# Layer 2 of a four-layer attention stack: probabilities turned by TensorE, or split into 16-bit planes and turned by a DMA

## The reference

```python
xq = _layernorm(q, ln1_w, ln1_b)
Q = jnp.einsum('btc,hdc->bhtd', xq, Wq)
K = jnp.einsum('bsc,hdc->bhsd', k, Wk)
V = jnp.einsum('bsc,hdc->bhsd', v, Wv)
scores = jnp.einsum('bhtd,bhsd->bhts', Q, K) * D ** (-0.5)
wei = jax.nn.softmax(scores, axis=-1)
o = jnp.einsum('bhts,bhsd->bhtd', wei, V)
o = o.transpose(0, 2, 1, 3).reshape(q.shape[0], q.shape[1], H * D)
q1 = q + o @ Wproj.T + bproj
h = _layernorm(q1, ln2_w, ln2_b)
return q1 + jax.nn.relu(h @ W1.T + b1) @ W2.T + b2
```

## Time and profile before

| | |
|---|---|
| Median of 3 runs | 4999.22 us (4997.36 to 5001.67) |
| The profiled execution | 5001.85 us, span 5000.1 us |
| PE / PEld busy | 4600.5 us (92%) / 3401.8 us (68%) |
| DVE / ACT / POOL busy | 2935.6 us (59%) / 2821.5 us (56%) / 2007.6 us (40%) |
| Mean granted TensorE clock | 0.957 |
| DMA queue q1 | 279216 packets, 155.99 MB, 12.9% of 16 engines |

### The profile page before, as it was taken

The page is one execution under the profiler, slowest core; times in us unless marked ns, Lnnn a source line. Parts: engine busy times, 40 slices in busy tenths (PEclk is TensorE's granted clock), DMA queues, the critical chain, the costliest instruction groups (busy, mean ns, idle before and its releaser), DMA issues.

```text
span 5000.1 us, 86857 instructions
## 1 busy us (share of the span) xinstructions
PE 4600.5 (92%) x32032; PEld 3401.8 (68%) x32032; DVE 2935.6 (59%) x6466; ACT 2821.5 (56%) x8969; POOL 2007.6 (40%) x3876
## 2 busy tenths in 40 slices
PE   8999999876877777789999999999999999999998
PEld 5666666655656556567777777777777777777777
DVE  6566556566656665664544454445445766676665
ACT  4555555688888888863333333333334666666664
POOL 3333333466565665642222222222223444444443
PEclk9999999988889888899999999999999999999999
DMA  2000000133333333331000000000000100000000
GB/s 82 21 24 21 25 23 21 51 67 62 64 62 61 62 67 56 68 69 39 11 14 14 14 11 14 14 14 11 14 23 23 37 15 21 21 18 16 20 17 7
DMA packets 279638, 161.54 MB, mean 32 GB/s; under 512 B 244528, under 2 KB 261168, under 8 KB 277808
## 3 DMA queue, kind: packets, MB, share of 16 engines
q1 hardware_dynamic: 279216, 155.99, 12.9%
HBM read 82.53 MB, written 14.68 MB: 19 GB/s over the span
## 4 chain that ended last, share of the span: by engine, by line
PE 83%; ACT 8%; POOL 3%; DVE 2%; issue 2%; DMA 2%; SPq 0%; ACTq 0%; POOLq 0%; DVEq 0%
PE ring L1340 49%; PE ring L1287 11%; PE score L1273 11%; ACT e L1460 5%; PE ring L1322 3%; PE ring L1315 3%; PE ring L1329 2%; DMA probs<-steps 2%; POOL e L1850 1%; PE ring L1284 1%; POOL e L1847 1%; PE ring L1305 1%; ACT work L1521 1%; PE ring L1355 1%; DVE nmax L1595 1%
## 5 line engine op out<-in xcount | busy, mean ns | idle before, releaser
L1850 POOL TENSOR_SCALAR e<-e,rsum 112x375 f32<-112x375 f32 (+1 forms) x2048 | 1067.4, 540 | 2214.8 <-DVE rsum L1602 2178.9
L1500 ACT COPY probs<-ring 125x336 f32<-125x336 f32 (+1 forms) x971 | 400.1, 448 | 1648.2 <-PE ring L1287 1533.9
L1595 DVE TENSOR_REDUCE nmax<-score 112x2 f32<-112x750 f32 (+1 forms) x1152 | 1064.7, 951 | 420.6 <-PE score L1273 420.5
L1460 ACT ACTIVATE e<-score,nmax 112x375 f32<-112x375 f32 (+1 forms) x2048 | 1039.1, 539 | 42.5 <-DVE nmax L1595 38.2
L1340 PE MATMUL ring<-h,weights 128*128 128x224 f32 x3840 | 876.0, 369 | 30.0 <-ACT work L1521 24.9
L1273 PE MATMUL score<-keys,q 64*112 64x375 f32 (+2 forms) x3584 | 608.4, 494 | 232.4 <-ACT e L1460 229.6
L1340 PEld LDWEIGHTS ring<-h,weights 128*128 128x128 f32 x3840 | 724.9, 197 | 104.4 <-ACT work L1521 33.7
L1287 PEld LDWEIGHTS ring<-consts,e 112*125 112x125 f32 x4608 | 584.5, 188 | 230.8 <-issue 178.9
L1287 PE MATMUL ring<-consts,e 112*125 112x112 f32 x4608 | 645.4, 279 | 4.6 <-POOL e L1850 2.6
L1340 PE MATMUL ring<-weights,ctx 128*125 128x512 f32 (+3 forms) x1536 | 588.4, 516 | 0.0
L1273 PEld LDWEIGHTS score<-keys,q 64*112 64x112 f32 (+2 forms) x3584 | 233.0, 166 | 509.2 <-ACT e L1460 287.1
(11 more groups left out here) (123 smaller groups left out, 5104.9 us busy)
## 6 DMA issues: line engine op xcount, KB each, us to landing
ctx<-ctx_t SPq DMA_DIRECT2D x128, 375.0 KB, 3.1
out_t<-x SPq DMA_DIRECT2D x64, 224.0 KB, 1.9
x<-out_t SPq DMA_DIRECT2D x48, 224.0 KB, 2.6
weights<-weights SPq DMA_DIRECT2D x7, 1024.0 KB, 6.2
probs<-steps SPq DMA_TRANSPOSE x320, 2.7
x<-x_t SPq DMA_DIRECT2D x16, 224.0 KB, 2.6
weights<-weights SPq DMA_DIRECT2D x1, 3328.0 KB, 12.3
weights<-weights SPq DMA_DIRECT2D x1, 2304.0 KB, 9.4
```

Of the source, the lines that this page charges most:

```text
L1460: ins = nc.scalar.activation(e_of(u)[:, n * width:(n + 1) * width], score_bank(u)[0:S, n * width:(n + 1) * width], ACT.Exp, bias=minus, sc ...
L1500: ins = nc.scalar.copy(dst, src)
L1595: ins = dve.tensor_reduce(to, src, AX, ALU.max, negate=True)
L1850: ins = nc.gpsimd.tensor_scalar(mine, mine, rsum[0:S, slot(u), n:n + 1], 0.0, ALU.mult, ALU.add)
```

## The change

In layer 2 the turns on TensorE are gone. After `weigh`, a new step `split` on GpSimd (L1946 of the changed kernel, two instructions for each pair) reads the float32 probabilities as pairs of 16-bit words and writes all low halves and all high halves into `halves`, three slots of 12 blocks of 128 columns. A transposing DMA on SyncE's queue (L1996) moves the 12 blocks into `planes`, two slots. A new step `merge` on VectorE (L1734) or ScalarE (L1537) interleaves the two planes again into float32 words in `probs`. The context is cut into chunks of 128, 128 and 119 keys in place of three of 125, in `cv` and in `pv`. Layer 1's `steps` now share their memory with `halves`, which is cleared once at the start as `steps` was.

```diff
+WORDS = (2, )
+SPLIT_BY = ("G",)
+SPLITS = 3
+PLANES = 2
...
-                if o.layer != 1:
+                if o.layer != 1 and not self.in_words(o):
                     self.turn_of[u] = self.job(p.index + lag + 0.1 * i, "turn", o.layer, o.s, o.b, 0, "VA", u)
             if p is o.pairs[-1] and len(o.pairs) == (2 if o.attn == "self" else 4):
-                self.pv_of[o] = self.job(p.index + (3.4 if o.layer == 1 else lag + 0.5), "pv", o.layer, o.s, o.b, o.half, PV_BY[o.layer], o)
+                self.pv_of[o] = self.job(p.index + (3.4 if o.layer == 1 else (4.5, 0, 3.9, 4.3)[o.layer] if self.in_words(o) else lag + 0.5), "pv", o.layer, o.s, o.b, o.half, PV_BY[o.layer], o)
+    def halves_before(self, p):
+
+        i = self.nth_halved[p]
+        found = [self.halved[i - SPLITS]] if i >= SPLITS else []
...
+    def in_words(self, o):
+        return o.layer in WORDS and o.attn == "cross"
...
+            if self.in_words(o_):
+                by = SPLIT_BY[self.nth_halved[p] % len(SPLIT_BY)]
+                self.add("split", p, by, 1.7, p.index + 1.4)
+                self.add("flip", p, "D", 4.2, p.index + 1.6)
+                self.add("merge", p, "VA", 1.45, p.index + 2.4)
...
+        elif kind == "split":
+            yield "weigh", x
+            for p in self.halves_before(x):
+                yield "flip", p
+        elif kind == "merge":
+            yield "flip", x
+            for o in self.probs_before(x.octet):
+                yield "job", self.pv_of[o]
+        elif kind == "flip" and self.in_words(x.octet):
+            yield "split", x
+            i = self.nth_halved[x]
+            if i >= PLANES:
+                yield "merge", self.halved[i - PLANES]
...
-        steps = sb("steps", [P, STEPSLOTS, 8 * P], BF16)
+        halves = sb("halves", [P, SPLITS, 4 * CHUNKS * P], U16)
+        steps = halves[:, :, :].rearrange("p a n -> p (a n)")[:, 0:STEPSLOTS * 8 * P].bitcast(BF16).rearrange(
+            "p (a n) -> p a n", a=STEPSLOTS)
+        planes = sb("planes", [P, PLANES, 4 * CHUNKS * S], U16)
...
+        def split(eng, wait, p):
+            wait.wait_ge(weighed, nth["weigh", p])
+            for before in plan.halves_before(p):
+                flip_done(wait, before)
+            to = halves_of(p).rearrange("p (h a n) -> p h a n", h=2, a=2)
+            src = e[0:S, pair_slots(p), 0:T].bitcast(U16).rearrange("p a (n h) -> p h a n", h=2)
+            return [(to[:, h, :, 0:T], src[:, h, :, :]) for h in range(2)]
+
+        def merge(wait, p):
+            flip_done(wait, p)
+            wait.done([plan.pv_of[o] for o in plan.probs_before(p.octet)])
+            to = merged_of(p).rearrange("p a n -> p (a n)").bitcast(U16).rearrange("p (m h) -> p m h", h=2)
+            return to, planes_of(p).rearrange("p (h m) -> p m h", h=2)
...
-            return (P * c, min(T, P * c + P)) if layer == 1 else (R * c, R * c + R)
+            return (P * c, min(T, P * c + P)) if layer == 1 or layer in WORDS else (R * c, R * c + R)
...
+                elif kind == "merge":
+                    to, src = merge(wait, x_)
+                    nc.scalar.copy(to, src).then_inc(merged["A"], 1)
...
+                elif plan.in_words(before.octet):
+                    wait.wait_ge(halved[plan.split_by[before]], nth["split", before])
...
+                elif kind == "merge":
+                    to, src = merge(wait, x_)
+                    dve.tensor_copy(to, src).then_inc(merged["V"], 1)
...
+                if kind == "split":
+                    for to, src in split(pool, wait, x_):
+                        ins = nc.gpsimd.tensor_scalar(to, src, 1.0, 0.0, ALU.mult, ALU.add)
+                    ins.then_inc(halved["G"], 1)
+                    continue
...
+                        sp.dma_start(planes_of(p).rearrange("p (a n) -> p a n", n=S), halves_of(p),
+                                     transpose=True).then_inc(turned[n % FLIPS], 16)
```

More of the change, by code:

```diff
@@ L224, in place_attention @@
         self.turn_of, self.pv_of = {}, {}
+        self.halved = [p for p in self.pairs if self.in_words(p.octet)]
+        self.nth_halved = {p: i for i, p in enumerate(self.halved)}
         self.ones = [p for p in self.pairs if p.octet.layer == 1]
@@ L481, in before @@
                     yield "eight", self.pairs[x.index - ES // 2]
+                elif self.in_words(self.pairs[x.index - ES // 2].octet):
+                    yield "split", self.pairs[x.index - ES // 2]
                 else:
@@ L828, in arrange @@
                     step.x.clip_by, step.x.clip_nth = e, counts[e, "clip"]
+                if step.kind == "merge":
+                    self.by[step.x] = e
+                if step.kind == "split":
+                    self.split_by[step.x] = e
                 if step.kind == "job":
@@ L1078, in probs_of @@
             dt = BF16 if o.layer == 1 else F32
-            if o.layer == 1 and not is_own(o):
-                return part(probs[:, o.index % 2, :], 0, [8, CHUNKS, S], dt)[chunk_rows(1, c), col, c, :]
+            if o.layer == 1 and not is_own(o) or plan.in_words(o):
+                return part(probs[:, o.index % 2, :], 0, [8, CHUNKS, S], dt)[chunk_rows(o.layer, c), col, c, :width]
             if is_own(o):
@@ L1295, in tensor_heads @@
                     flip_done(wait, p)
+            elif plan.in_words(o):
+                for p in o.pairs:
+                    wait.wait_ge(merged[plan.by[p]], nth["merge", p])
             else:
@@ L1372, in tensor_product @@
                     half, c = j.m // 3, j.m % 3
-                    return product(ps[0:R, :], ((src[:, k, c * R:(c + 1) * R], wt[:, k, half * 512:half * 512 + 512])
-                                                for k in range(KC)))
+                    a, z = chunk(2, c)
+                    return product(ps[0:z - a, :], ((src[:, k, a:z], wt[:, k, half * 512:half * 512 + 512])
+                                                    for k in range(KC)))
                 for i, c in enumerate((0, 1) if j.m == 0 else (2,)):
@@ L1624, in vector_program @@
                     ins.then_inc(ctx_scaled, 1)
+                elif kind == "split":
+                    for to, src in split(dve, wait, x_):
+                        ins = dve.tensor_copy(to, src)
+                    ins.then_inc(halved["V"], 1)
+                elif kind == "merge":
+                    to, src = merge(wait, x_)
+                    dve.tensor_copy(to, src).then_inc(merged["V"], 1)
                 elif kind == "eight":
@@ L1627, in vector_program @@
                     wait.wait_ge(weighed, nth["weigh", p])
-                    i = plan.nth_of_one[p]
-                    if i >= STEPSLOTS:
-                        flip_done(wait, plan.ones[i - STEPSLOTS])
+                    for before in plan.steps_before(p):
+                        flip_done(wait, before)
                     if is_own(p.octet):
@@ L1875, in sync_program @@
                     n = nth["flip", p] - 1
+                    if plan.in_words(p.octet):
+                        wait.wait_ge(halved[plan.split_by[p]], nth["split", p])
+                        i = plan.nth_halved[p]
+                        if i >= PLANES:
+                            before = plan.halved[i - PLANES]
+                            wait.wait_ge(merged[plan.by[before]], nth["merge", before])
+                        sp.dma_start(planes_of(p).rearrange("p (a n) -> p a n", n=S), halves_of(p),
+                                     transpose=True).then_inc(turned[n % FLIPS], 16)
+                        continue
                     wait.wait_ge(stepped, nth["eight", p])
```

52 lines of the change are left out of this document (41 added, 11 removed).

## The result

The kernel with the change takes 4850.44 us (median of 4 runs, 4848.00 to 4852.07) against 4998.55 us for the kernel before on the same chip: ratio 0.9702 [0.9686, 0.9719], faster by 148 us. The forecast was 4838, with 4814 to 4890 as its range. The profiled execution took 4849.35 us, with a span of 4847.6, which is 152.5 us under the 5000.1 of before. One execution of one later experiment, the doubled split with its cost told to the plan, took 8945 us where its other three took 4848 to 4853; it is left out of that median, and as it was the profiled one, no rows of that run are shown.

A forecast was written before the change was run, and what follows sets the result against it. TensorE was taken to bound layer 2. From 5001.85 us, 172 off for turns, 9 added for stalls and 0.4 for clearing gave 4839.3; with the median 2.6 lower, 4836.7, stated as 4838, range 4814 to 4890.

The forecast's parts named there:

- The bound: Layer 2: TensorE, busy 1619.35 of 1620 us, bounds it, so whatever leaves TensorE there shortens the kernel.
- The turns: Layer 2: removing 512 turns from TensorE, 0.336 us each, saves 172 us, with 164 and 185 as ends.
- Stalls: Layer 2: saves standing behind long merges cost TensorE 0.6%, taken from layer 0's busy share: +9 us of 1448.
- The added work: Layer 2: splits of 0.93 us, DMAs landing after 3.9, merges of 1.58 (VectorE) or 1.28 (ScalarE), all hidden.
- Rival 1: Layer 2: merges waiting for DMAs block copies and stall TensorE, +79 us, 4906 us; milder form 4867; chance 0.19.
- Rival 2: Layer 2: splits make GpSimd the bound, slower than before from 2.47 us a split; 5830 us at 4.1; chance 0.03.
- Rivals 3 and 4: Layer 2: transposing DMA becomes the bound, slower from 6.33 us a pair (chance 0.02); or nothing is gained (0.03).
- Rival 4: Layer 2: the removed 172 us return as waits for scores and their exponentials, 4999 us; chance 0.03.

The follow-up runs named there:

- the run with 3.4: The changed kernel with layer 2's transposing DMA planned at 3.4 us in place of 4.2: 4848.33 us, 0.9697 of the kernel before.

## Why the prediction was right

**The bound (right).** TensorE alone bounded layer 2 before and does so after. What left it came off the time.

**The turns (the mis-sized term).** The forecast took 0.336 us each, 172 in all, between a start-to-start time (0.32) and the chain's share (0.36). The period of a stream gives 0.310, 158.7 in all. What a turn held was sized nearly right, 0.342 us by the timeline of before. The missed step is that not all of it leaves: 1.0 us a stream, 16 in all, comes back in the jobs that now stand next to scores and value products.

**Stalls (+9 forecast; none in the steady part).** TensorE is full from 2225 to 3610 us. Layer 0's 0.6% was no fit measure for it. Instead the seam lost 6.8 us, which no step foresaw. That these two errors nearly cancel is luck. In full: 158.7 off TensorE, less 6.8 at the seam, is 151.9, where the spans differ by 152.5. From the forecast: 13.3 us of turns too much, 9 of stalls too many, 6.8 for the seam missing, and the median 1.1 us over the profiled execution and not 2.6 under it, +3.7, bring 4836.7 to 4851.5; measured were 4850.4.

**The added work (hidden, as forecast).** Splits 0.83 us (0.93 forecast), DMAs landing after 3.5 (3.9), ScalarE's merges 1.46 (1.28). VectorE's merges take 0.85, not 1.58; even the lower end of 1.02 was too high. The choice to price a strided read "as slowly as anything here" had no row behind it. It cost nothing, since VectorE had room. Clearing `halves` takes 3.94 us against 3.51, +0.4 as forecast.

**Rival 1 (right as a mechanism, not here).** It decides on the plan, not on load: the DMA lands after 3.5 us and is planned at 4.2. Planned at 2.0 the same kernel loses 86 us. The merges' waits of 98 us did not reach TensorE, and of 409 us of them in the run with 3.4 it lost 1.3.

**Rival 2 (right as a limit).** It put the edge at 2.47 us a split, for the time of the kernel before. Three splits, 2.58 us in sum by their mean in that run, give 5309, 6% slower. The sign is right, but GpSimd's 6.46 us a pair account for about 30 of those 307 us. The plan still had 1.7 us for the three, and what a true cost would give back there was not run. Two splits, planned rightly, cost nothing, as the rival's arithmetic has it.

**Rivals 3 and 4 (wrong).** Twelve blocks land in 3.5 us, under 5.65. From six to twelve blocks the landing grows by 0.8 us, 0.13 a block. The Trainium skill ("VectorE: DVE Perf Modes", "The three transpose paths") gives 1309 ns for one block, from which the prediction estimated 15.7 us for twelve. The trace does not bear that out: a DMA's blocks do not go one after another at that price. Rival 4's waits for scores would show as gaps of TensorE, and from 2225 to 3610 us there is none.

## What to carry to other kernels

Price an operation on a full engine by the difference of a period that recurs, or by start to next start where its neighbours are of its kind; a share of the chain also holds switches that stay. Moving work to other engines pays only where these have room for it and the order has room for its latency: the same change gave 148 us in layer 2 and made layer 0 41 us longer. The chain alone does not tell which it is: GpSimd held 65% of it in the doubled split, and a true cost in the plan made that loss vanish. In an order fixed from planned costs, check the planned time of each long step against the trace first; a DMA told 1.5 us too short cost 86 us, and one told 0.7 too long cost nothing that these runs show. And compare the stages that the edit did not touch: the new order made layer 1 50 us longer in a run that changed layer 0.

## What the runs showed of the hardware

- A copy of 1344 words of 16 bits between two SBUF tiles, the source read with a stride, takes 0.85 us on VectorE and 1.46 on ScalarE. 750 such words on GpSimd take 0.83.
- A transposing DMA of twelve blocks lands 0.8 us after one of six would (3.5 and 2.7), and holds the queue 0.15 us longer (1.36 and 1.21).
- GpSimd's instructions vary in their mean, and how busy the other engines are does not by itself set it. The weighing of 375 elements takes 595 ns in layer 2 before, 634 after, 599 in the doubled split, 609 in layer 0 with half of its octets and 695 with all of them; in the last two VectorE is busy 62% and 61%, ScalarE 58% and 60%. The median split stays at 829 to 831 ns while its mean is 831 in the change and up to 911 in the doubled split, so a part of them is much longer. The cause was not isolated.
- Where TensorE has gaps its mean granted clock falls below 1.00: 0.97 with two splits, 0.91 with three, 0.93 in layer 0 with the change. Idle time alone does not set it: 61 us of it in 1200 go with 0.97, and 56 with 0.99. Part of these losses is the clock's: with two splits a stream's work takes TensorE 93.5 us, where it takes 90.4 at 1.00.
- A job of four matmuls on 128 by 128 weights and 375 columns holds TensorE for 1.27 us next to its like, and 1.36 to 1.37 next to value products.
